# GLA attention with a mixture of experts: the gate on the attention output moves to the head of a round, the multiply by the inverse rms goes behind it on GpSimd

## The reference, cut to what matters

```python
o = o * rsqrt(mean(o * o, axis=-1, keepdims=True) + EPS) * g_norm_weight
o = o * (g * sigmoid(g))
return o.reshape(b, n, h * dv) @ Wo
...
x = _layernorm(x + attention(x))
x = _layernorm(x + expert_layer(x))
```

## Time and profile before

| | us |
|---|---|
| median of 3 runs | 231.29 |
| lowest and highest | 229.92, 232.61 |
| the profiled execution | 230.26 |
| its span, first to last instruction | 228.3 |
| the rounds 2 to 18 in it | 44 to 113 |
| mean granted TensorE clock, as a share of full speed | 0.926 |

### The profile page before, as it was taken

One profiled execution on the slowest core, in us unless ns is written; L12 is line 12 of the kernel. 1 busy time (PEld: TensorE's weight loads), 2 busy tenths in 40 slices (PEclk: granted clock), 3 DMA queues, 4 the chain that ended last, 5 costly groups with the idle time before them and its releaser, 6 DMA issues.

```text
span 228.3 us, 5556 instructions
## 1 busy us (share of the span) xinstructions
PE 180.0 (79%) x1428; PEld 142.5 (62%) x1428; DVE 149.7 (66%) x519; ACT 120.1 (53%) x384; POOL 107.6 (47%) x129
## 2 busy tenths in 40 slices
PE   2999969697887898988580879999999999993000
PEld 1656623364664665756480869999899999992000
DVE  5389992967889777577832455666666666662284
ACT  1188595536566566666443046565565555561155
POOL 6090040424418775686673724554455544455360
PEclk9999999999999999999557699999999999999555
DMA  6999999999802921101122322222221220000653
GB/s 171 282 195 205 215 186 214 213 169 204 271 18 65 304 73 31 46 31 40 46 74 59 96 69 67 65 72 71 65 78 51 71 74 23 32 9 1 219 217 115
DMA packets 33870, 25.72 MB, mean 113 GB/s; under 512 B 3310, under 2 KB 29604, under 8 KB 33840
## 3 DMA queue, kind: packets, MB, share of 16 engines
q1 hardware_dynamic: 30624, 20.96, 43.0%
q0 software_dynamic: 2272, 4.24, 5.2%
q10 hardware_dynamic: 944, 0.17, 0.4%
HBM read 11.03 MB, written 14.79 MB: 113 GB/s over the span
## 4 chain that ended last, share of the span: by engine, by line
PE 47%; DVE 19%; issue 10%; ACT 8%; another core or an unknown queue 5%; DMA 5%; POOL 3%; ACTq 1%; SPq 1%; DVEq 0%; POOLq 0%
PE psum L1392 15%; PE psum L1377 14%; DMA gate<-expert_results 2%; DVE cum_and_q L775 2%; DVE v_sb L761 2%; DVE xr L921 2%; PE psum L1294 2%; PE psum L1188 2%; PE psum L1366 2%; PE psum L1331 2%; DVE gT L770 2%; PE psum L1201 2%; PE psum L1172 2%; PE psum L1327 1%
## 5 line engine op out<-in xcount | busy, mean ns | idle before, releaser
L531 POOL DMA_INDIRECT expert_results<-kT,xg x39 | 38.5, 987 | 41.9 <-issue 26.6
L1392 PE MATMUL psum<-w_sb,gT 128*128 x312 | 45.0, 288 | 6.4 <-ACT gT L680 6.2
L680 ACT ACTIVATE gT<-psum,b_sb 128x128 f32<-128x128 f32 x117 | 34.6, 365 | 23.4 <-issue 17.9
L1377 PE MATMUL psum<-kT,km 128*128 128x128 f32 x312 | 44.1, 287 | 1.6 <-ACT kT L666 1.6
L1392 PEld LDWEIGHTS psum<-w_sb,gT 128*128 128x128 f32 x312 | 38.8, 196 | 10.4 <-issue 9.1
L1377 PEld LDWEIGHTS psum<-kT,km 128*128 128x128 f32 x312 | 40.5, 203 | 1.8 <-ACT kT L666 1.7
L501 POOL DMA_INDIRECT expert_rows<-xr,slot x32 | 31.4, 980 | 12.7 <-issue 9.6
L1038 DVE COPY km<-cum_and_q 128x512 f32 x39 | 17.0, 436 | 17.1 <-PE psum L1377 10.8
L496 POOL TENSOR_TENSOR rgate<-rrms,gate 128x256 f32<-128x256 f32 x16 | 12.5, 780 | 22.1 <-ACT rrms L621 21.0
L666 ACT ACTIVATE kT<-psum 128x128 f32<-128x128 f32 x39 | 10.8, 277 | 21.2 <-PE psum L1366 12.7
L1056 DVE TENSOR_TENSOR kT<-psum,b_sb 128x128 f32<-128x128 f32 x39 | 11.4, 291 | 13.0 <-issue 7.0
(11 more groups left out here) (178 smaller groups left out, 342.8 us busy)
## 6 DMA issues: line engine op xcount, KB each, us to landing
expert_rows<-pad_row SPq DMA_DIRECT2D x8, 1105.0 KB, 17.5
xg<-expert_rows SPq DMA_DIRECT2D x39, 65.0 KB
cum_and_q<-in_L_ffn_W_dram SPq DMA_DIRECT2D x8, 256.0 KB
gate<-expert_results SPq DMA_DIRECT2D x8, 256.0 KB, 5.6
x_sb<-in_L_attn_x_dram SPq DMA_DIRECT2D x4, 256.0 KB, 4.1
out_dram<-x_sb SPq DMA_DIRECT2D x8, 128.0 KB, 2.0
expert_results<-kT,xg POOLq DMA_INDIRECT x39
b_sb<-in_L_ffn_b_dram SPq DMA_DIRECT2D x1, 512.0 KB, 16.2
```

The lines of the kernel that those rows point to most:

```text
L531: pool.indirect_dma_start(out=results[:, :], in_=yw[:, u, :], in_offset=None, bounds_check=TOP * N - 1, oob_is_err=False, out_offset=bass. ...
L680: act.activation(hT[:, h, n, :], bank[2 * (i % 2)][:, n * P:(n + 1) * P], ACT.Relu, bias=b1_sb[:, bass.ds(e * HC + n, 1)]).then_inc(s_hTa, 1)
L1377: last = mm(bank[2 * (i % 2) + half][:, k * P:(k + 1) * P], w1_buf[u][:, n * P:(n + 1) * P], xgT[:, h, :], start=True, stop=True)
L1392: last = mm(out_bank(i)[:, 0:D], hT[:, h, n, :], w2_all[:, bass.ds(first + n * D, D)], start=(n == 0), stop=(n == HC - 1))
```

## The change

`gate_o` on DVE now multiplies `o` from PSUM by `gate` instead of `rgate`, and stands at the head of a round, behind `mask_scores`. It waits for the squares of that tile (ACT must have read `o` too, since the bank is free for PE once `s_og` is raised) and for the projection two tiles back (which has read this half of `ogT`). POOL's stage is now `gated_over_rms`: it waits for `s_og` and for the inverse rms and multiplies `ogT` in place by `rrms`. `project_out` on PE waits for POOL's semaphore instead of DVE's. The tile `rgate` goes.

```diff
-        rgate = sb("rgate", [P, 2, DVC, P])
...
-            def gate_over_rms(t):
+            def gated_over_rms(t):
+                pool.wait_ge(s_og, t + 1)
                 pool.wait_ge(s_rr, t + 1)
-                if t >= 2:
-                    pool.wait_ge(s_og, t - 1)
-                pool.tensor_tensor(rgate[:, t % 2, :, :], rrms[:, t % 2, :, :], gate[:, :, t * P:(t + 1) * P],
-                                   ALU.mult).then_inc(s_rg, 1)
+                pool.tensor_tensor(ogT[:, t % 2, :, :], ogT[:, t % 2, :, :], rrms[:, t % 2, :, :], ALU.mult).then_inc(s_rg, 1)
...
             def gate_o(t):
-                dve.wait_ge(s_rg, t + 1)
+                dve.wait_ge(s_sq, t + 1)
+                if t >= 2:
+                    dve.wait_ge(s_dve_bank, t - 2 + AGE_OUT)
                 dve.tensor_tensor(ogT[:, t % 2, :, :], bank[4 + t % 2][:, 0:DV].rearrange("p (c t) -> p c t", t=P),
-                                  rgate[:, t % 2, :, :], ALU.mult).then_inc(s_og, 1)
+                                  gate[:, :, t * P:(t + 1) * P], ALU.mult).then_inc(s_og, 1)
...
                 take(mask_scores, 0)
+                take(gate_o, AGE_GATE)
                 take_batch(count_hits, placing)
...
                 take_batch(find_max, scored)
-                take(gate_o, AGE_GATE)
                 take_batch(find_index, scored)
...
             def project_out(t):
-                pe.wait_ge(s_og, t + 1)
+                pe.wait_ge(s_rg, t + 1)
```

More of the change, by code:

```diff
@@ L246, in build @@
         s_rr = sem("rrms_done")
-        s_rg = sem("gate_over_rms_done")
+        s_rg = sem("gated_o_over_rms_done")
         s_og = sem("o_gated")
@@ L508, in _ @@
                 if t is not None:
-                    gate_over_rms(t)
+                    gated_over_rms(t)
                 if i in groups_ended:
```

## The result

| | before | after |
|---|---|---|
| first measurement, median of 4 | 230.6 (227.57 to 232.61) | 233.07 (231.44 to 234.84) |
| second measurement (`after_again`), median | 232.04 (17 executions) | 232.31 (12 executions) |
| the profiled execution | 230.26 | 233.74 |
| its span | 228.3 | 231.7 |
| mean granted clock in it | 0.926 | 0.894 |

The first measurement gave a ratio of 1.0188 with a 95% interval of 1.0109 to 1.0267, about 4 us more, where 1.06 us had been forecast. That ratio compares only executions within 1.5% of the fastest of their kernel, which leaves two of the four of before (227.57 and 229.92) and all four of after; over all eight the means are 230.35 and 233.10, 2.75 us apart. The second, with 17 executions of before and 12 of after, gave 1.0017 (0.9968 to 1.0065).

A forecast was written before the change was run, and what follows sets the result against it. The attention rounds were taken as bound by a ring from TensorE's transpose through residual, statistics, rstd and normalize. Terms +0.40, +0.36 and +0.30 sum to +1.06 us on 231.29: 232.3 us, range 230.0 to 234.3.

The forecast's parts named there:

- from that the forecast is 231.29 + 1.06: Whole kernel: the summed terms added to the median of the runs shown of before, giving 232.3 us, 0.5% longer.
- Term 1, round 5: +0.40: Round 5: mask and residual run back to back on DVE, so the gate in front moves everything behind it, +0.40 us.
- Term 2, round 8: +0.36: Round 8: later gate delays GpSimd's multiply and first scatter, and the normalize ends with that scatter, +0.36 us.
- Term 3, rounds 12 and 14: +0.30: Rounds 12 and 14: mask released late, so the gate ends later and GpSimd starts later, +0.15 us each.
- rival B: Even rounds: the old gate did hold the normalize, so removing it gains 1.1 us, or 2.0 without late releases; chance 0.20.
- Round 18: 0: Round 18: L1294 can start 0.8 us earlier, but DVE's residual behind its copy does not hang on it, 0.
- The port step: Even rounds: GpSimd holds the shared port, so a normalize started inside its instruction ends 0.01 to 0.07 us after it.
- Rival C: Odd rounds: the second scatter gets ahead of the normalize and blocks it, +3.8 us with the forecast's terms; chance 0.17.
- Rival D: Whole kernel: the gate's place does nothing that lasts, no cost in rounds 5, 12 or 14, 231.3 us; chance 0.18.
- TensorE's 0 for the new wait: Rounds 3 to 17: L1294 comes over 1 us after GpSimd would be done, so waiting for GpSimd costs 0.
- rounds 4 and 7: Rounds 4 and 7: DVE is late, but ACT is later and the normalize ends with GpSimd's L486, 0.

The follow-up runs named there:

- after_again: The changed kernel, unedited, timed again beside more executions of before: median 232.31 us (12 executions), ratio 1.0017.
- split: The changed kernel with the DVE gate of rounds 5 and 8 alone moved behind the statistics: ratio 1.0098.
- defer_after: The changed kernel with all row scatters moved behind GpSimd's last multiply: 255.85 us, rounds 9 to 17 in 30.51 us.
- before_again: The kernel before, unedited, once more for a second trace: 233.01 us.
- paceall_before: The kernel before with a 128x512 memset and its wait ahead of each late row scatter and the first 12 result scatters: ratio 1.0186.
- pace_short: The kernel before with a 128x512 memset ahead of each late row scatter and a 128x32 one ahead of all result scatters but three: 230.83 us.
- pace2_after: The changed kernel with three memsets, each with its own wait, ahead of each late row scatter: 242.96 us, ratio 1.0647.
- defer_before: The kernel before with all row scatters moved behind GpSimd's last multiply: 254.78 us, rounds 9 to 17 in 30.52 us.
- thin_tail: The kernel before with the DVE gate cut to 4 of 128 columns of each half, most attention output left out: ratio 0.9963.
- pace_after: The changed kernel with one memset and its own wait ahead of each late row scatter: 230.61 us, ratio 1.0127.
- fill_before: The kernel before with up to six extra unread TensorE products a round in rounds 0 to 8: 238.75 us.
- fill_after: The changed kernel with up to six extra unread TensorE products a round in rounds 0 to 8: 236.3 us, ratio 1.0101.
- pace: Kernels before or changed, with memsets and waits put ahead of late scatters on GpSimd: 230.61 to 242.96 us where a time is given.
- pace_before: The kernel before with one memset and its own wait ahead of each late row scatter: 231.31 us, ratio 1.0119.

## Why the prediction was right and wrong

**The size.** Forecast 232.3 us, 0.5% over before; measured a ratio of 1.0188 at first, and 0.5 us with a standard error of 0.5 over all executions. The step that failed first is "from that the forecast is 231.29 + 1.06": a sum on the level of three executions of before, with no term for the clock. The text took before's profile (clock 1.00 in rounds 2 to 9) as the state that the changed kernel would have, and "about 1%, 2.3 us" as what a measurement resolves. The runs showed executions that spread by 2.3 us (standard deviation), so that the means of four and four differ by 1.6 us (one standard error) with no change at all. Of the 20 profiles of this study 17 have the clock at the lower level for 3.4 to 13.7 us somewhere between 46 and 90 us, with the change and without; the one of before that the prediction was read from is among the three that have not. The profile of after had 13.7 us of it, and its rounds were up to 5.8 us late. How much of the first 1.9% is clock and how much the draw of before cannot be told, since only one of its four executions of before has its clock on record.

The sum of 1.06 failed too. Its terms, one by one:

**Term 1, round 5: +0.40.** Right: 0.31 from mask to normalize, 0.37 over rounds 4 and 5.

**Term 2, round 8: +0.36.** Too large, and wrong in mechanism: 0.12 from mask to normalize, 0.20 over rounds 7 and 8. It was said to come through GpSimd, whose first scatter starts later and blocks the normalize. That scatter did start later, but the normalize was not blocked by it. In `split` the scatter comes behind the normalize, in `defer_after` there is none, and the round is as long. It is DVE's own chain.

**Term 3, rounds 12 and 14: +0.30.** Wrong in sign. The mask's late release was taken as given. In after it does not come in those rounds, and they are 0.2 to 0.3 us shorter each (in `before_again` round 12 has a late release at the residual instead). The text named the bound ("0 if the late release does not recur") but no gain below it; the gain stood under rival B. Round 11 gives part back with a later release of its own. Rounds 9 to 17 in all are 31.57 before (31.58 in `before_again`) against 30.99 and 31.21 after: -0.4 to -0.6.

**Round 18: 0.** It is 0.25 shorter, 2.67 instead of 2.92, but not by TensorE: DVE's copy, at 110.60 before, starts 0.84 us behind the normalize of round 17 in both. Before it starts 0.51 into GpSimd's scatter of 110.09 and takes 0.67; in `after_again`, 0.36 into it, it takes 0.43:

```profile
113.25 0.96 POOL L498 DMA_INDIRECT expert_rows<-xr,slot  x1 [0.30 <-issue]
...
113.61 0.43 DVE L1037 COPY km<-cum_and_q 128x512 f32 x1 [0.49 <-issue]
```

**Sum in the rounds.** 0.37 + 0.2 - 0.4 to -0.6 - 0.25 is -0.3 to 0.0. Straight from the profiles that have the full clock from round 3 to 16, from the normalize of round 3 to that of round 18: 61.85, 61.86 and 62.01 with the code of before (before, `paceall_before`, `pace_short`) against 61.81 and 61.57 with that of after (`after_again`, `pace2_after`); the pauses come in only at the end of this stretch. The pair with the same clock was 0.02 apart at round 18. So in place of +1.06 the rounds give nothing or a gain of up to 0.4, as costs and gains of 0.2 to 0.6 us that all but cancel.

**The port step** ("a normalize that starts inside a GpSimd instruction ends 0.01 to 0.07 after it, wherever it starts"; "Starting it earlier gains nothing"). Right for tensor_tensor: in round 4 of after L485 runs 58.67 to 59.94, the normalize starts at 58.91, takes 1.11 and ends at 60.02. Wrong for scatters. The rows of before had normalizes only at 0.49 and 0.62 us into one, and at 0.86 in round 8. In after round 14 starts 0.24 into its scatter and takes 0.35, round 10 0.03 into it and takes 0.34. The Trainium skill (SBUF — State Buffer, Who interferes with whom) has the port held for the whole instruction; the trace agrees for tensor_tensor and not for the indirect DMA.

**Rival B** came true in its sign, not in its cause or size. Normalizes of 0.33 to 0.35 us that end before the scatter does are there in rounds 8, 10 and 14 of after, and rounds 12 and 14 got shorter. But the gate did not hold them: with no scatters the even rounds take 3.78 us with it in either place (`defer_before`, `defer_after`), and thinning it out gave 0.2 us (`thin_tail`). What after gains in rounds 9 to 17 is part of the 1.05 us that the scatters cost before. **Rival C** falls: where an odd normalize did start behind a scatter's start, it was not blocked (0.08 into it in round 15 of `pace_after`, 0.35 long). **Rival D**, no effect, is nearest to what all executions together show, though for other reasons: it had no late releases in 12 and 14 but no cost in 5 either. TensorE's 0 for the new wait held, and rounds 4 and 7 end within 0.1 us of where they did.

**What was not foreseen** is that 1.6 us came back behind round 18 in the first profile of after. The prediction said "Nothing after round 18 should take it up or add to it." Each profile has three waits there, of 4.9, 6.0 and 6.9 us in before and 4.1, 6.1 and 5.4 in after. The first of these two lines is the third wait of before, the second that of after:

```profile
132.22 0.28 ACT L666 ACTIVATE kT<-psum 128x128 f32<-128x128 f32 x1 [6.91 <-remote]
...
135.78 0.28 ACT L663 ACTIVATE kT<-psum 128x128 f32<-128x128 f32 x1 [5.39 <-PE psum L1365]
```

Up to the second wait nothing came back: it ends 10.93 us behind the normalize of round 18 in before (123.61) and 10.98 in after (128.69). The third ends 19.54 behind it in before and 18.07 in after, and there the 1.5 us are. It isn't a gain of the change: in `after_again` it is 19.09, and in `fill_before` and `fill_after` 19.65 and 19.69. The `pace` kernels show that these waits come from GpSimd's runs of scatters; why the third was short in this one profile is open.

## What to carry to other kernels

Before you explain a difference of 1 or 2%, lay the rows of granted clock of the two profiles side by side, and take more executions if they differ; here a low draw of before and a profile of after with the clock low for 13.7 us made a change of about nothing look like +1.9%. When an operation is split between two engines, cost the order of the factors and the place of the instruction apart: the new factors in the old place cost 3%, in the new place nothing that could be measured. And where a wait ends a fixed distance behind another engine's instruction, look at that instruction first, even if it is not named as the releaser.

## What the runs showed of the hardware

- An indirect DMA on GpSimd (0.95 to 1.01 us long) slows VectorE's tensor_scalar only in part of its time. By how far into the scatter the normalize started: 0.03 to 0.34 us, 0.33 to 0.35 us long; 0.41 to 0.43, 0.56 to 0.58 (once 0.35); 0.49 to 0.51, 0.53 to 0.54; 0.57 to 0.70, 0.34 to 0.43; 0.79 and later, 0.33 to 0.35. Each slowed one ended 0.02 to 0.03 us behind the scatter. In the first scatter of round 8, 1.19 us long, a normalize that started at 0.64 was not slowed (0.33).
- TensorE's releases to ACT and DVE arrive late around such scatters: 0.5 to 0.65 us behind the end of one, and often only at the end of a run of them 1.26 to 1.29 us apart (0.17, 0.28 and 0.31 us behind it in `paceall_before`, before and after; 1.37 in `pace_before`, 1.9 in `pace2_after`), after waits of up to 10.5 us. With 0.8 us between two scatters they come through. It is shown that spacing removes the waits and that they follow the run wherever it goes; what in the chip holds them is not. Nor is it a strict rule: in round 12 of after ACT's rms starts at 93.06, inside the scatter at 92.30, and in `pace_before` a release came through at 142.44, in the middle of a run.
- Added matmuls in rounds 0 to 8 did not keep the clock from falling at 47 us.
